# Decay mixing with a routed low-rank layer: eviction places, the third group's router, and two orders in the first batch

## The reference, cut to what matters

```python
decay = exp(-exp(w)) * (0.5 + 0.5 * tf)         # per channel; tf from cond, per batch
ek = exp(min(f, 30)); ekv = ek * f              # k and v are both f
nf, df = forward scans  of ekv, ek:  a = a * decay + input
nb, db = backward scans of ekv, ek
euk = exp(min(u + f, 30))
num = nf + nb - ekv + euk * f
den = df + db - ek + euk
y = sigmoid(x) * num / max(den, 1e-8) * (0.8 + 0.2 * tf)

h = silu(y @ rw1.T + rb1)                       # 64 hidden features
logits = (h @ rw2.T + rb2)[:, :16] + gates
coeff = softmax over the two best logits, 0 for the other experts
xa = y @ A                                      # 16 experts x rank 16 = 256 features
out = x + y @ W.T + bias + (xa * coeff) @ B
```

## Time and profile before

| | |
|---|---|
| median of 3 runs | 682.92 us |
| profiled execution, device time | 682.46 us |
| its span, first to last instruction | 680.4 us |
| PE busy | 591.8 us (87%) |
| DVE busy | 520.8 us (77%) |
| ACT busy | 360.2 us (53%) |
| POOL busy | 367.8 us (54%) |
| mean granted PE clock | 0.957 of full speed |

### The profile page before, as it was taken

One profiled execution on the slowest core, in us unless ns is written; L12 is line 12 of the kernel. 1 busy time (PEld: TensorE's weight loads), 2 busy tenths in 40 slices (PEclk: granted clock), 3 DMA queues, 4 the chain that ended last, 5 costly groups with the idle time before them and its releaser, 6 DMA issues.

```text
span 680.4 us, 6882 instructions
## 1 busy us (share of the span) xinstructions
PE 591.8 (87%) x2546; PEld 477.2 (70%) x2546; DVE 520.8 (77%) x579; ACT 360.2 (53%) x428; POOL 367.8 (54%) x183
## 2 busy tenths in 40 slices
PE   0153688879999936999999999999999999999997
PEld 0132576658878824788888887888788888888786
DVE  7999899998989999999879996999699322021202
ACT  6777899854765668457735574567454221011100
POOL 1789998866878777557535854485456401000100
PEclk9966799989999967999999999999999999999999
DMA  5324477525664832135413442326222402040122
GB/s 193 123 91 153 143 232 206 180 94 109 167 158 90 207 105 93 47 113 174 162 47 108 147 164 77 109 105 204 77 78 78 154 1 72 21 153 2 28 65 78
DMA packets 33249, 78.45 MB, mean 115 GB/s; under 512 B 4736, under 2 KB 4928, under 8 KB 33216
## 3 DMA queue, kind: packets, MB, share of 16 engines
q1 hardware_dynamic: 30912, 73.82, 33.2%
q0 software_dynamic: 2304, 4.20, 4.3%
HBM read 57.03 MB, written 20.97 MB: 115 GB/s over the span
## 4 chain that ended last, share of the span: by engine, by line
PE 65%; DVE 16%; POOL 6%; ACT 6%; issue 4%; DMA 3%; SPq 0%; POOLq 0%; ACTq 0%; DVEq 0%
PE acc L915 21%; PE acc L917 20%; PE acc L916 20%; DVE mix L726 3%; DVE mix L721 2%; DVE mix L747 2%; DVE mix L717 2%; DMA out<-xo 2%; DVE eu L736 2%; PE acc L926 1%; PE acc L927 1%; DVE yr L753 1%; DMA xo<-w_router_a 1%; PE acc L964 1%; POOL y_lo L624 1%
## 5 line engine op out<-in xcount | busy, mean ns | idle before, releaser
L915 PE MATMUL acc<-y_hi,wa_hi 128*128 128x512 f32 x640 | 259.2, 405 | 57.5 <-POOL y_lo L624 50.8
L916 PE MATMUL acc<-y_lo,wa_hi 128*128 128x512 f32 x640 | 255.0, 398 | 0.0
L917 PE MATMUL acc<-y_hi,wa_lo 128*128 128x512 f32 x640 | 254.6, 398 | 0.0
L915 PEld LDWEIGHTS acc<-y_hi,wa_hi 128*128 128x128 f32 x640 | 123.7, 193 | 90.4 <-POOL y_lo L624 52.2
L917 PEld LDWEIGHTS acc<-y_hi,wa_lo 128*128 128x128 f32 x640 | 123.5, 193 | 26.8
L916 PEld LDWEIGHTS acc<-y_lo,wa_hi 128*128 128x128 f32 x640 | 123.8, 193 | 24.9
L614 POOL TENSOR_TENSOR mix<-mix,kv 128x1024 f32<-128x1024 f32 x31 | 74.3, 2396 | 93.8 <-DVE mix L705 78.7
L760 DVE SCALAR_TENSOR_TENSOR xo<-acc,bias_sb,xo 128x512 f32<-128x512 f32 x64 | 46.7, 737 | 75.9 <-PE acc L917 75.7
L624 POOL TENSOR_TENSOR y_lo<-yr,y_hi 128x1024 fp32r<-128x1024 f32 x31 | 76.4, 2466 | 35.0 <-ACT y_hi L401 34.7
L637 POOL TENSOR_TENSOR wx_lo<-xa,wx_hi 128x512 fp32r<-128x512 f32 x16 | 20.8, 1318 | 118.4 <-ACT wx_hi L478 118.4
L726 DVE TENSOR_TENSOR_SCAN mix<-d_ps,mix 128x1023 f32<-128x1023 f32 x32 | 74.7, 2334 | 3.6 <-ACT mix L413 3.6
(11 more groups left out here) (105 smaller groups left out, 696.8 us busy)
## 6 DMA issues: line engine op xcount, KB each, us to landing
kv<-f_cm SPq DMA_DIRECT2D x32, 512.0 KB, 3.5
yr<-x_cm SPq DMA_DIRECT2D x32, 512.0 KB, 3.5
out<-xo SPq DMA_DIRECT2D x64, 256.0 KB, 3.3
xo<-x_cm SPq DMA_DIRECT2D x64, 256.0 KB, 3.7
out<-xo POOLq DMA_DIRECT2D x16, 256.0 KB, 6.0
xa<-w_base SPq DMA_DIRECT2D x5, 512.0 KB, 3.6
xo<-w_base SPq DMA_DIRECT2D x3, 512.0 KB, 6.1
xo<-w_router_a SPq DMA_DIRECT2D x2, 480.0 KB, 3.8
```

What stands on the lines that cost most here:

```text
L915: nc.tensor.matmul(out_ap, wh, yh, start=start, stop=False)
L916: nc.tensor.matmul(out_ap, wh, yl, start=False, stop=False)
L917: return nc.tensor.matmul(out_ap, wl, yh, start=False, stop=stop)
```

## The change

It has five parts.

1. The table of evictions of groups 0 and 1: tiles 0, 2, 4 to 7, 14 and 15 each move one place or more back. Group 1's `routing` moves behind `forward_num`, its `weigh` behind `backward_den`.
2. Group 2 (SPLIT): its router no longer spreads over steps 16 and 17. `hidden`, `silu` and `routing` all go into step 16 on DVE, ahead of `backward_num`; ACT's `low_rows`, `copy_xa`, `sigmoid_z` and later `exp_gap`, `copy_turned` too, behind `exp_k(17)`; `weigh` comes right after the ratio in step 17, and ACT's and POOL's `split_wx` soon after. PE does four blocks of tile 1 ahead of the logits, and blocks of tile 2 around `turn` and `spread`.
3. `scale_e` has only the scalar form; the copy of its factors into PSUM goes.
4. For units 1 to 7, ACT does `scale_end_den` ahead of the sigmoid and its table load.
5. POOL, unit 15: `gate_late` moves ahead of `sum_n`, and `split_late_lo` ahead of `gate_n`.

```diff
--- before.py
+++ after.py
         (AFTER_RATIO, AFTER_FWD, AFTER_FWD_NUM, AFTER_BWD_DEN, AFTER_SUM, AFTER_BWD_NUM) = range(6)
-        evacs_at = {(CB + 2, AFTER_RATIO): (0, 1), (CB + 2, AFTER_FWD): (1, 3), (CB + 2, AFTER_FWD_NUM): (3, 5),
-                    (CB + 2, AFTER_BWD_DEN): (5, 6), (CB + 2, AFTER_BWD_NUM): (6, 7), (CB + 3, AFTER_RATIO): (7, 8),
+        evacs_at = {(CB + 2, AFTER_FWD): (0, 2), (CB + 2, AFTER_FWD_NUM): (2, 4), (CB + 2, AFTER_BWD_DEN): (4, 5),
+                    (CB + 2, AFTER_BWD_NUM): (5, 6), (CB + 3, AFTER_RATIO): (6, 7), (CB + 3, AFTER_FWD_NUM): (7, 8),
                     (CB + 4, AFTER_BWD_NUM): (8, 10), (CB + 5, AFTER_FWD): (10, 12), (CB + 5, AFTER_FWD_NUM): (12, 13),
-                    (CB + 5, AFTER_BWD_DEN): (13, 14), (CB + 5, AFTER_SUM): (14, 15),
-                    (CB + 5, AFTER_BWD_NUM): (15, 16)}
+                    (CB + 5, AFTER_BWD_DEN): (13, 14), (CB + 5, AFTER_BWD_NUM): (14, 15),
+                    (CB + 6, AFTER_FWD): (15, 16)}
         AFTER_GATE, AFTER_LO = range(2)
...
                 late_split, late_sigmoid = held(s - 1), held(s - 2)
-                if q == 1:
+                third = s == first_step(SPLIT)
+                if q == 1 and G != SPLIT:
                     sigmoid_z(G)
...
                     exp_uk(s)
-                if q == 1:
+                if q == 1 and G != SPLIT:
                     copy_xa(G)
...
                     split_hi(s - 1)
-                if s < UNITS and q != 1 and not late_sigmoid:
+                if 0 < s < CB:
+                    scale_end_den(s)
+                if q == 1 and G == SPLIT:
+                    split_wx(G)
+                if third:
+                    scale_end_num(s)
+                    exp_k(s + 1)
+                    low_rows(G)
+                    copy_xa(G)
+                    sigmoid_z(G)
+                if s < UNITS and (q != 1 or G == SPLIT) and not late_sigmoid:
                     sigmoid_r(s)
-                if s < UNITS and s - 1 not in HALVED:
+                if s < UNITS and s - 1 not in HALVED and not 0 < s < CB:
                     if s == 0:
...
                     scale_end_den(s)
-                if q == 1:
+                if q == 1 and G != SPLIT:
                     exp_gap(G)
...
                     split_hi(s - 1)
-                if q == 1:
+                if q == 1 and G != SPLIT:
                     copy_turned(G)
-                if s < UNITS and q != 1 and not late_sigmoid:
+                if s < UNITS and (q != 1 or G == SPLIT) and not late_sigmoid:
                     exps()
-                if s < UNITS:
+                if third:
+                    exp_gap(G)
+                if s < UNITS and not third:
                     scale_end_num(s)
-                if s + 1 < UNITS:
+                if s + 1 < UNITS and not third:
                     exp_k(s + 1)
...
                         drain_part(p)
-                if q == 1:
+                if q == 1 and G != SPLIT:
                     split_wx(G)
...
                     exps()
-                if q == 0:
+                if q == 0 and G != SPLIT:
                     low_rows(G)
...
                     inverse(s)
+                if third:
+                    copy_turned(G)
                 for n in chunks_at(hi_steps, s):
...
                     sum_late(s - 1)
+                    gate_late(s - 1)
                 if 0 < s <= UNITS:
...
                 if s - 1 in HALVED:
-                    gate_late(s - 1)
+                    split_late_lo(s - 1)
                 if 0 < s <= UNITS:
...
                 if s - 1 in HALVED:
-                    split_late_lo(s - 1)
                     split_lo(s - 1)
+                if q == 1 and G == SPLIT:
+                    split_wx(G)
                 for e in tiles(adds_at, s, AFTER_GATE):
...
                     weights_lo(n)
-                if q == 1:
+                if q == 1 and G != SPLIT:
                     split_wx(G)
...
                 dve.wait_ge(ek_ready, g + 1)
-                if 0 < g <= CB:
-                    nc.vector.scalar_tensor_tensor(out=den_of(g), in0=den_of(g), scalar=EXP30, in1=decay(UNITS + g, T),
-                                                   op0=ALU.min, op1=ALU.mult).then_inc(e_scaled, 1)
-                else:
-                    nc.vector.tensor_scalar(den_of(g), den_of(g), EXP30, delta_f[:, g:g + 1],
-                                            ALU.min, ALU.mult).then_inc(e_scaled, 1)
+                nc.vector.tensor_scalar(den_of(g), den_of(g), EXP30, delta_f[:, g:g + 1],
+                                        ALU.min, ALU.mult).then_inc(e_scaled, 1)
 
...
             link(nc.vector.tensor_copy(d_ps[:, 0:UNITS], d_g[:, :, :].rearrange("p b c -> p (b c)")))
-            link(nc.vector.tensor_copy(d_ps[:, UNITS:2 * UNITS], delta_f))
 
...
                 first_groups(s, AFTER_RATIO)
-                if q == 1:
+                third = s == first_step(SPLIT)
+                if q == 1 and G == SPLIT:
+                    weigh(G)
+                if q == 1 and G != SPLIT:
                     silu(G)
...
                     evacuate(ended, 5)
-                if q == 1:
+                if q == 1 and G not in (1, SPLIT):
                     routing(G)
...
                     dve.wait_ge(rbg_ready, 1)
-                if q == 1:
+                if q == 1 and G == 1:
+                    routing(G)
+                if q == 1 and G not in (1, SPLIT):
                     weigh(G)
...
                     backward_den(s)
+                if q == 1 and G == 1:
+                    weigh(G)
                 first_groups(s, AFTER_BWD_DEN)
+                if third:
+                    hidden(G)
                 if ending:
...
                 first_groups(s, AFTER_SUM)
+                if third:
+                    silu(G)
                 if s + 1 < UNITS:
                     scale_e(s + 1)
-                if q == 0:
+                if third:
+                    routing(G)
+                if q == 0 and not third:
                     hidden(G)
...
                         base(G, 0, kc)
+                ahead = 4 if G == SPLIT else 0
+                if ahead:
+                    bank_in(G, 4)
+                    for kc in range(ahead):
+                        base(G, 1, kc)
                 if G != 1:
...
                 bank_in(G, 4)
-                for kc in range(k0, CB):
+                for kc in range(max(k0, ahead), CB):
                     base(G, 1, kc)
...
                     pe.wait_ge(constants_ready, 2)
+                if G == SPLIT:
+                    pe.wait_ge(xa_copied, 2 * G + 1)
+                    for kc in range(3):
+                        base(G, 2, kc)
                 turn(G)
...
                 if G:
-                    for kc in range(k0, k0 + 3):
+                    for kc in range(3 if G == SPLIT else k0, 5 if G == SPLIT else k0 + 3):
                         base(G, 2, kc)
...
                 if G:
-                    for kc in range(k0 + 3, CB):
+                    for kc in range(5 if G == SPLIT else k0 + 3, CB):
                         base(G, 2, kc)
...
                     pe.wait_ge(wx_ready, 2 * G + a + 1)
```

## The result

The median went from 684.12 us (22 runs, 681.63 to 688.22) to 681.13 us (22 runs, 679.83 to 683.67): a ratio of 0.9956, 95% interval [0.9943, 0.9970]. The gain of 3.0 us is real, and under 1%. The profiled execution of the changed kernel took 681.20 us (span 679.3, granted clock 0.962) against 682.46 (span 680.4, clock 0.957). So the two traces differ by 1.26 us, not 3.0: the traced run of before lies 1.7 under its median, the traced run of after on its own.

The account below looks back on a forecast made before the run. TensorE, fully busy from 300 us, bounds the kernel, held before that by DVE's evictions at tile 5 of group 2. Upstream gains shrink to -1.3 us, +1.4 for lost clock makes zero: 682.5 us, range 676.5 to 687.5.

Parts of the forecast that it names:

- What bounds the kernel: From 300 us TensorE is fully busy at 2.4 GHz; only an edit letting it enter that stretch sooner shortens the program.
- Parts 1 and 2: Steps 0 to 7: 7.2 us offered by step 8, ACT takes it back; gain 1.0 at step 9, ends -4.7 and +7.2.
- rival c: Scalar form held by GpSimd in all eight scaling steps: 4.7 us lost, 687.4 us; chance 0.1.
- Part 3: Evictions of groups 0 and 1: 3.4 us of DVE waits go; step 14's second scan at 226.4, gain 3.6 us.
- Part 4: Unit 15: GpSimd's second-half subtraction moves ahead of a 1.26 us instruction; TensorE's start goes from 259.01 to 254.2 us.
- Part 5: Group 2's router: first eviction 289.2 against 290.42, leaving 1.2 to 1.4 us gain; TensorE idles 4 us at tile 5.
- The sum: -1.3 us left plus 1.4 for TensorE's lower clock after the idle time is zero: 682.46 becomes about 682.5.

Follow-up runs that it names:

- no_scalar: The changed kernel with the scaling of units 1 to 8 in its old two-tensor form; 682.07 us, ratio 0.9960 to the kernel before.
- no_end_first: The changed kernel with the end corrections of steps 1 to 7 behind the sigmoid again; 683.26 us, ratio 0.9988 to the kernel before.
- early_tile0: The changed kernel with group 2's first three evictions one place sooner on VectorE; 678.30 us, ratio 0.9904 to the kernel before.
- third_only: The kernel before with the sooner router of group 2 alone; 687.84 us, ratio 1.0043 to the kernel before.
- first_batch_only: The kernel before with only the scalar form and the end corrections ahead of the sigmoid in steps 1 to 7; 681.29 us, ratio 0.9951.
- early_fed: early_tile0 with two blocks of base products (6 matmuls) of group 0's tile 1 ahead of its logits on TensorE; 677.25 us, ratio 0.9887 to the kernel before.
- evict_only: The kernel before with the later eviction places and group 1's moved router alone; 681.63 us, ratio 0.9953 to the kernel before.
- third_filled: The changed kernel with p2 and unit 16's numerator backward scan ahead of the hidden layer's DVE instruction; 681.56 us, ratio 0.9962 to the kernel before.
- filled_early2: The changed kernel with third_filled's order in step 16 and group 2's first three evictions where VectorE passes them soonest; 677.90 us, ratio 0.9884 to the kernel before.

## Why the prediction was right

The forecast was no change (682.5, range 676.5 to 687.5); the measured gain is 3.0 us, inside the range and under 1%. The range was 11 us wide, nearly four times the gain, so the hit says little by itself; the sum gave no change, and what it explains is the traced pair (1.1 us), not the 3.0 of the medians. That the number stands is in part luck. Step by step:

- **What bounds the kernel**: right, and the table makes it sharper. Only the start of group 3 counts.
- **Parts 1 and 2**: the mechanism was right, the size wrong. I took 0.5 by step 8 and 1.0 by step 9; the pair of traces gives 2.1 and 2.6. I was right that ACT's chain ends step 7 (no_scalar), but read its floor from the chain of before, whose wait for a store had its own lateness in it. The chain came sooner as a whole: the exponential that started at 117.28 starts at 116.03. Of DVE's 3.6 us of waits for end corrections 0.6 is left, and up to 125 us DVE has 3.8 us of new waits, 2.5 for ACT's exponentials and 1.3 for GpSimd's product.
- **The scalar form beside GpSimd** (rival c): it did not come in the changed kernel; without part 2 it came in two steps (no_end_first). The 32 scalings take 739 to 1794 ns, and 23 of them meet no GpSimd instruction at all, those of steps 0, 1, 2 and 7 among them. In batch 0 the four others take 0.75 to 1.13. I had GpSimd still at work when the scaling comes, and priced it at 1.80; it is at work, but near the end of an instruction, and only what is left of that one is waited for. The Trainium skill (GPSIMD Engine Reference, 8. Key points) says that GpSimd contends with DVE instructions in a two-port mode, and gives no price there; here both sides paid, 0.39 and 0.45 us.
- **Part 3**: the eviction waits went, as forecast, but for a wait of 1.04 for tile 6's load of x that I had not seen. The weighing came at 196.48 (197.95 forecast) and the scan of step 14 at 224.96 (226.4), both early by what batch 0 gave more.
- **Part 4**: unit 15 at 252.94 (254.2). No run has part 4 alone or undone alone, but the traces give its size: from the start of ratio 15 to unit 15 on TensorE pass 6.20 or 6.21 us in the four kernels without it and 5.16 or 5.17 in the ten with it, so 1.0 (1.2 forecast).
- **Part 5**: DVE's wait in the routing of 4 us (3.60 + 0.79), GpSimd's split of the gated rows (1.60, forecast 1.6), the eviction at 288.04 (289.2), the wait of some 4 us at tile 5 (3.64) and the lower clock behind it (1.6, forecast 1.4) are all in the trace. early_tile0 shows that they are causes: with the eviction sooner, wait and fall go and 3 us come back.
- **The sum**: forecast 0 for the profiled pair, measured -1.1. The difference is the 1.2 to 1.6 us that batch 0 gave more.

What I had not argued is how the parts stand to each other. Parts 1 and 2 alone give 0.9951, part 3 alone 0.9953, part 5 alone 1.0043, parts 1 to 4 together 0.9964, all 0.9956. The first two overlap nearly whole: both bring unit 15 forward, and once it comes at 252.9 the next limit takes 5 us back, in these traces, at the hidden layer or at tile 5.

Open: why the medians differ by 3.0 and the traces by 1.3. The runs of before spread wider (681.6 to 688.2 against 679.8 to 683.7). A fall of the clock in step 9 costs 2.0 us there. From ratio 8 to ratio 15 pass, with the new eviction places, 116.9 to 117.9 us in the traces without that fall and 117.4 to 118.2 in those with it; with the old places 119.4 and 119.5 without, 120.5 and 120.9 with it. So some of it is recovered by ratio 15, and how much depends on more than the places. If the fall is commoner or dearer in the kernel before, the medians differ by more than the traced pair; only one execution of it was traced, so that isn't shown. The same gap is there the other way round in third_only (traces 6.4 us apart, 2.9 by the ratio) and in part 3's gain within the change (3.5 by the medians, 2.6 by the traces).

## What to carry to other kernels

Find the point behind which the bounding engine never waits again, and measure every edit by when that engine gets there; here the start of group 3 gave the span of thirteen of fourteen traces to 0.1 us. An advance upstream is worth only what the next bank, buffer or router lets through, so look for the instruction that frees it and ask whether its engine could do it one place sooner: moving three evictions that cost nothing gave as much again as the whole change. Test parts alone and left out; two that each give 3 us may give 3 us together.

## What the hardware showed that I had not expected

- TensorE's clock after a wait, in these traces: kept after 1.47 us (early_tile0, tile 5), and after 2.26 and 2.43 (logits of group 2 in first_batch_only and in the kernel before); fallen after 2.84 (early_fed, tile 5), 2.94 (the same logits in evict_only), 3.64 and 3.61 (tile 5), 4.70 and 5.62 (logits), 5.37 (tile 5 of third_filled), but also after 2.15 (group 3 of filled_early2). After 1.50 to 1.55 us ahead of group 0's logits both were seen: kept in seven kernels, fallen in six, with the same work in front of it. In six of those seven it fell some 10 us later, behind two waits of 0.77 and 0.75, and the step was not longer for it. So the length of the last wait does not decide alone. Behind the falls listed by their waits 7 to 13 matmuls stand at 0.43 in place of 0.23, 1.4 to 2.6 us.
- A scalar form of DVE that starts inside a GpSimd instruction ends 0.55 us after that one ends. Of the 416 scalings in this form in the fourteen traces 105 start so, and all of them end 0.546 to 0.558 after it; the other 311 take 0.73 to 0.76. So it is in the earlier trace rows and, in the changed kernel, at 199.94, 309.65, 382.79 and 453.78 us. The last, GpSimd's timeline and then DVE's (452.62 + 2.41 = 455.03; 453.78 + 1.79 = 455.57):

```profile
452.62 2.41 POOL L639 TENSOR_TENSOR y_lo<-yr,y_hi 128x1024 fp32r<-128x1024 f32 x1 [1.17 <-ACT y_hi L401]
```

```profile
453.78 1.79 DVE L718 TENSOR_SCALAR mix<-mix,delta_g 128x1024 f32<-128x1024 f32 x1
```

- The same rule covers one that starts at the boundary between two GpSimd instructions: it waits for the short one in which it starts, not for the next. At 71.21 that one ends at 71.79, and the scaling 0.55 later, after 1.13 us. The next GpSimd instruction then pays: 2.28 in place of 1.83. The old form, with its factor in PSUM, took 1.21 in all eight steps, three of them beside a GpSimd instruction, and that instruction took 1.83 at 58.51 and at 73.15.
